# Set-up of a two-layer transformer kernel: seven staging buffers, block 0's attention first, later weight strips beside block 0's MLP

## The reference

```python
# layer 0
h = ada_rms(x, cond, ln1_w, ln1_tw)        # x*rsqrt(mean x^2) * w*(1 + cond @ tw.T)
q, k, v = h@Wq.T, h@Wk.T, h@Wv.T           # 8 query heads of 64, one k/v head
q, k = rope(q), rope(k)
x = x + softmax(q k^T / 8) v @ Wo.T
h = ada_rms(x, cond, ln2_w, ln2_tw)
x = x + (silu(h@Wg.T) * (h@Wu.T)) @ Wd.T   # 2048 inner
# layer 1
gamma1, gamma2, scale1, scale2, shift1, shift2 = silu(cond) @ Wada.T + bada
x = x + attn(ln(x)*(scale1+1)+shift1) * gamma1      # 16 heads of 32, unit q and k
x = x + (gelu(( ln(x)*(scale2+1)+shift2 )@Wfc1.T + bfc1)@Wfc2.T + bfc2) * gamma2
```

## Time and profile before

| | |
|---|---|
| runs | 2766.93, 2768.59, 2770.6 us (median 2768.59) |
| profiled execution, its own time | 2764.49 us |
| its span, first to last instruction | 2762.7 us |
| mean granted TensorE clock | 0.969 |
| TensorE busy | 2524.8 us, 91% |
| VectorE, ScalarE, GpSimd busy | 1395.9, 962.3, 1040.4 us |
| TensorE by 40 slices of 69 us | 2449999999999999999997769999999999999998 |
| granted clock by slice | 9669999999999999999999889999999999999999 |

### The profile page before, as it was taken

How to read it: one execution, slowest core, us unless ns; L and a number is a source line. 1 busy time by engine, 2 the same in 40 slices (tenths; PEclk the granted TensorE clock), 3 DMA queues, 4 the chain that set the end, 5 groups by cost and what they waited for, 6 DMA issues and landing times.

```text
span 2762.7 us, 47260 instructions
## 1 busy us (share of the span) xinstructions
PE 2524.8 (91%) x18552; PEld 1255.8 (45%) x18552; DVE 1395.9 (51%) x2115; ACT 962.3 (35%) x1549; POOL 1040.4 (38%) x1007
## 2 busy tenths in 40 slices
PE   2449999999999999999997769999999999999998
PEld 1224445454444444444443335454454545454543
DVE  4554434243342524435224657575767667575742
ACT  2332213132231322223122336262626354444532
POOL 1112223132231322223121546564655555565632
PEclk9669999999999999999999889999999999999999
DMA  6430010100001010010205111212121112112110
GB/s 201 132 98 3 7 45 3 50 3 28 26 5 48 3 46 7 12 40 4 76 3 179 36 43 29 74 31 76 28 66 44 55 42 60 48 45 65 32 54 27
DMA packets 115019, 129.40 MB, mean 47 GB/s; under 512 B 53758, under 2 KB 56190, under 8 KB 114820
## 3 DMA queue, kind: packets, MB, share of 16 engines
q1 hardware_dynamic: 114820, 126.36, 15.2%
HBM read 71.79 MB, written 18.87 MB: 33 GB/s over the span
## 4 chain that ended last, share of the span: by engine, by line
PE 73%; issue 10%; DVE 7%; POOL 5%; ACT 4%; DMA 0%; POOLq 0%; SPq 0%; DVEq 0%; ACTq 0%
PE ps_m L1440 38%; PE ps_abef L1440 18%; PE ps_d L1440 2%; PE ps_c L1440 2%; PE ps_abef L1619 2%; PE ps_abef L1621 2%; PE ps_abef L1626 2%; PE ps_abef L1653 1%; PE ps_d L1607 1%; POOL h_mlp L815 1%; POOL inner L837 1%; POOL scratch L868 1%; PE ps_abef L1642 1%; PE ps_abef L1661 1%; PE ps_c L1475 1%
## 5 line engine op out<-in xcount | busy, mean ns | idle before, releaser
L1440 PE MATMUL ps_m<-h_mlp,weights 128*128 128x512 f16 x3072 | 708.5, 383 | 38.9 <-POOL h_mlp L815 19.1
L1440 PE MATMUL ps_m<-weights,inner 128*128 128x512 f16 x3072 | 690.4, 379 | 8.7 <-DVE scratch L1280 8.7
L1440 PEld LDWEIGHTS ps_m<-h_mlp,weights 128*128 128x128 f16 x3072 | 296.8, 99 | 384.9 <-issue 38.4
L1440 PEld LDWEIGHTS ps_m<-weights,inner 128*128 128x128 f16 x3072 | 296.9, 98 | 346.1 <-DVE scratch L1280 6.5
L837 POOL TENSOR_TENSOR inner<-scratch,inner 128x512 f16<-128x512 f32 x256 | 301.0, 1176 | 315.6 <-ACT inner L1000 315.6
L1440 PE MATMUL ps_abef<-h_mlp,weights 128*128 128x512 f16 x1536 | 345.4, 379 | 0.0
L1440 PEld LDWEIGHTS ps_abef<-h_mlp,weights 128*128 128x128 f16 x1536 | 147.6, 98 | 173.0
L806 POOL TENSOR_TENSOR scratch<-scratch 128x1 f32<-128x1 f32 x128 | 29.1, 228 | 434.3 <-ACT scratch L945 379.1
L1000 ACT CAST inner<-scratch 128x512 f16<-128x512 f32 x256 | 156.6, 612 | 101.6 <-DVE scratch L1408 68.1
L815 POOL TENSOR_TENSOR h_mlp<-scratch,h_mlp 128x512 f16<-128x512 f32 x64 | 74.0, 1156 | 199.2 <-ACT h_mlp L958 199.2
L1278 DVE SCALAR_TENSOR_TENSOR scratch<-scratch,ps_m 128x512 f32<-128x512 f32 x64 | 44.0, 688 | 198.2 <-ACT scratch L1008 198.2
(11 more groups left out here) (169 smaller groups left out, 3646.3 us busy)
## 6 DMA issues: line engine op xcount, KB each, us to landing
x_mlp<-x_attn SPq DMA_DIRECT2D x64, 256.0 KB, 2.3
weights<-gamma SPq DMA_DIRECT2D x128, 128.0 KB, 2.9
scratch<-scratch SPq DMA_DIRECT2D x128, 128.0 KB, 2.6
x_attn<-x SPq DMA_DIRECT2D x32, 256.0 KB, 2.7
x_mid<-x_mlp SPq DMA_DIRECT2D x32, 256.0 KB, 2.0
x_attn<-x_mid SPq DMA_DIRECT2D x32, 256.0 KB, 2.7
out<-x_mlp SPq DMA_DIRECT2D x32, 256.0 KB, 2.2
inner<-wada_t SPq DMA_DIRECT2D x6, 1024.0 KB, 5.9
```

The source lines that it names most:

```text
L1440: ins = nc.tensor.matmul(o, left(a, k), right(b, k), start=(first and n == 0), stop=(last and n == len(order) - 1), skip_group_check=True)
```

## The change

It replaces the order of set-up by two tables, `SETUP_AT` (by slot of block 0's attention) and `START_AT` (by slot of block 0's MLP), whose pieces each engine takes at the head of a slot.

- Block 0's attention has a table of its own, `FIRST0`, with 20 slots: proj of the tiles in slots 2, 5, 8, 11, norm2 in 13, 15, 17, 19.
- Seven staging buffers: i0 to i3 in `inner`, b0 to b2 in the space of `down_w`, and the fourth quarter of that space for the modulation's results.
- The ada strips aren't cut. TensorE multiplies them in fp32, right from the staging buffer, into four PSUM banks in turn.
- The first eight sequences' gains are written straight into `gains`, and the rope rows of block 0 into `rope`. The angles are worked out in four parts (4, 8, 10 and 10 of 32 columns of 32).
- gate2, up2, gate3, up3 and down0 to down3 are cut in slots 1 to 8 of block 0's MLP; TensorE waits for each pair of up and gate strips only where it needs it, and ScalarE waits for all cuts before chunk 8, which overwrites i1.
- Loads wait by buffer, x has one semaphore a tile, POOL makes the frequencies first.

```diff
+GROUPS0 = ["tw0", "qkv", "qkv_v", "tw1", "wo", "gate0", "up0", "ada4", "ada5", "ada6", "ada7", "ada2", "ada3",
+           "gate1", "up1", "gate2", "up2", "gate3", "up3", "down0", "down1", "down2", "down3"]
+STAGED0 = ["i0", "i1", "i2", "i3", "b0", "b1", "b2", "i0", "i1", "i2", "i3", "b0", "b1",
+           "b2", "i1", "i3", "b0", "b1", "b2", "i1", "i3", "i1", "i3"]
+ADAS = [0, 1, 4, 5, 6, 7, 2, 3]
+SETUP_AT = {
+    0: [("ang", 0)],
+    1: [("sin", 0), ("ang", 1), ("ada", 0)],
+    2: [("cut", "qkv"), ("cut", "qkv_v"), ("store", 0), ("load", "gate0"), ("rope", 0), ("sin", 1), ("ang", 2)],
+    3: [("rope", 1), ("load", "up0"), ("sin", 2), ("load", "ada4"), ("ada", 1), ("store", 1)],
+    4: [("rope", 2), ("load", "ada5"), ("ang", 3), ("sin", 3)],
+    5: [("cut", "wo"), ("load", "ada6"), ("ada", 4), ("store", 4)],
+    6: [("rope", 3), ("load", "ada7"), ("ada", 5), ("store", 5)],
+    7: [("rope_out", 0), ("load", "ada2"), ("cut", "gate0"), ("ada", 6), ("store", 6)],
+    9: [("load", "ada3"), ("ada", 7), ("store", 7)],
+    10: [("cut", "up0"), ("ada", 2), ("store", 2)],
+    11: [("load", "gate1"), ("load", "up1"), ("load", "gate2")],
+    12: [("load", "up2"), ("ada", 3), ("store", 3)],
+    13: [("load", "gate3")],
+    18: [("cut", "gate1")],
+    19: [("cut", "up1")],
+}
+START_AT = {
+    0: [("load", "up3")],
+    1: [("cut", "gate2"), ("load", "down0")],
+    2: [("cut", "up2"), ("load", "down1")],
+    3: [("cut", "gate3")],
+    4: [("cut", "up3")],
+    5: [("cut", "down0")],
+    6: [("load", "down2"), ("cut", "down1")],
+    7: [("load", "down3"), ("cut", "down2")],
+    8: [("cut", "down3")],
+}
...
             def ada(n):
-                pe.wait_ge(s_wlo, g + 1)
...
-                    for f in range(KC):
-                        ins = products([(bank[:, NSEQ * f:NSEQ * (f + 1)], lambda b, k: c[:, b, k, :])],
-                                       lambda a, k: ada_cut[:, a, k, P * f:P * (f + 1)], range(KC))
+                    for f in range(KC):
+                        for k in range(KC):
+                            ins = nc.tensor.matmul(bank[:, NSEQ * f:NSEQ * (f + 1)], staged(g)[:, k, P * f:P * (f + 1)],
+                                                   c[:, k, :], start=(k == 0), stop=(k == KC - 1))
...
-            for s in range(SLOTS0):
-                for stage, t in TABLE0[s]:
+            for s in range(FIRST_SLOTS):
+                setup(SETUP_AT.get(s, ()))
+                for stage, t in FIRST0[s]:
                     attn0(stage, 0, t)
-                if FIRST + s < SETUP:
-                    setup_group(FIRST + s)
-            pe.wait_ge(s_wlo, SETUP)
+            pe.wait_ge(s_ada_out, len(ADAS))
...
+                            if first_block(it) and j % 4 == 0:
+                                pe.wait_ge(s_wlo, cut_no(no_of(f"up{j // 4}")))
...
+                if L is L0 and first_block(it) and j == IC // 2:
+                    act.wait_ge(s_wlo, cut_no(SETUP - 1))
```

More of the change, by code:

```diff
@@ L70, with table0 @@
                     [2, 6, 10, 14], [0, 4, 8, 12], [1, 5, 9, 13], [16, 18, 20, 22], [17, 19, 21, 23])
+FIRST_SLOTS = 20
+FIRST0 = slot_table(FIRST_SLOTS, ["proj", "turn", "scores", "softmax", "turn_p", "mix", "out"],
+                    [2, 5, 8, 11], [0, 3, 6, 9], [1, 4, 7, 10], [12, 14, 16, 18], [13, 15, 17, 19])
+def table0(it):
+    return FIRST0 if isinstance(it, int) and it == 0 else TABLE0
 def order_of(table, stages):
@@ L648, in _ @@
+            load_x(L0, x, 0, 0)
+            sp.dma_start(ln_w_t, ln_w).then_inc(s_lnw, 16)
+            for name in ("tw0", "qkv", "qkv_v"):
+                load_group(no_of(name))
+            for t in range(1, TILES):
+                load_x(L0, x, 0, t)
+            sp.dma_start(b_ada_t, b_ada).then_inc(s_bada, 16)
             for n in range(2):
-                sp.dma_start(b_ada_bc[n], b_ada_row[n:n + 1, :].to_broadcast([NSEQ, D])).then_inc(s_setup_dma, 16)
+                sp.dma_start(gamma_row[n], b_ada_row[n:n + 1, :].to_broadcast([NSEQ, D])).then_inc(s_bada, 16)
@@ new lines, in setup @@
+            def setup(pieces):
+                for piece, which in pieces:
+                    if piece == "load":
+                        load_group(no_of(which))
+                    if piece == "store":
+                        store_ada(which)
+                    if piece == "rope_out":
+                        sp.wait_ge(s_rope, len(ROPE_PARTS))
+                        rest = slice(TILES, NBLK * TILES)
+                        for which, table in ((0, cos_t), (1, sin_t)):
+                            sp.dma_start(rope_dram[:, rest, which, :],
+                                         table.rearrange("p (t f) -> p t f", f=32)[:, rest]).then_inc(s_rope_st, 16)
@@ L840, in _ @@
             pool.wait_ge(s_const, 43)
-            for s in range(SLOTS0):
-                for stage, t in TABLE0[s]:
+            for slot in FIRST0:
+                for stage, t in slot:
                     attn0(stage, 0, t)
@@ new lines, in setup @@
+            def setup(pieces):
+                for piece, which in pieces:
+                    if piece == "ang":
+                        angles(which)
+                    if piece == "rope":
+                        rotations(which)
+                    if piece == "ada":
+                        ada(which)
+                    if piece == "cut":
+                        cut_lo(no_of(which))
+            dve.wait_ge(s_pos, 16)
+            link(nc.vector.tensor_copy(pos_f, pos_i))
+            dve.wait_ge(s_const, 35)
```

384 lines of the change are left out of this document (196 added, 188 removed).

## The result

The changed kernel takes 2704.43 us (median of 4 runs, 2702.99 to 2707.65); the kernel before, run beside it, 2768.89 (4 runs, 2766.93 to 2770.6). The ratio is 0.9769, 95% interval 0.9752 to 0.9786. Forecast: 2707, range 2688 to 2727. The profiled execution took 2702.99 us, its span 2701.0 (before: 2762.7), so the spans differ by 61.7.

What follows compares the result with a forecast made beforehand. The prediction took TensorE's stream to bound the kernel, with set-up a hole at its front. Savings of 32.5 + 35 + 2 = 69.5 us, less 8, gave 61.5; from the 2768.6 median it forecast 2707, range 2688 to 2727.

Steps and rivals of the forecast that it cites:

- start, saved: Up to the first projection: it would start at 21.5 us in place of 54, saving 32.5.
- tile stretches, saved: Block 0's attention, proj of tile 0 to proj of tile 3: 106.0 us becomes 71, saving 35.
- tile 3 to the MLP, saved: Proj of tile 3 to block 0's MLP: 46.9 us becomes 45, counted as 2 saved.
- block 0's MLP, lost: Eight strips cut in slots 1 to 8 of block 0's MLP cost 8 us more.
- the rest: Per-tile x semaphores, renumbered cuts and waits of layer 1: long past events, so no cost.
- Price of the fp32 products: TensorE's ada products: between 1.8 and 9.1 us each, middle of 5.3 taken; 2.5 us not covered in the tile stretches.
- The lap: Block 0's MLP: ScalarE and VectorE's round per late cut takes 9.6 us against a slot's 6.8.
- A: Rival: the late cuts' relay binds at every slot of block 0's MLP, 22 us in place of 8; 15%.
- B: Rival: fp32 products dear, 9.1 us and more, adding 12 to 20 before the MLP; 15%.
- C: Rival: fp32 at its lower bound and late cuts hidden, total time 2688 to 2694 us; 14%.
- D: Rival: tiles keep their old pace of 34 to 36 us, only the start is won, 2744 us; 5%.
- E: Rival: slower than before, last strips arrive late, TensorE idle 8.7 us per strip decides; 2780 us if all eight; 2%.

Runs made afterwards that it cites:

- e1: Changed kernel with the cuts of qkv and its v columns moved ahead of ada0's finish and norm1 of tile 0: 2697.88 us, ratio 0.9744.
- e9: Changed kernel with the gains of block 0's first norm written to DRAM and loaded back again: 2710.7 us, ratio 0.9788.
- e10: Changed kernel with the fourth tile's angles, sine and rope row made in tile 2's slots: 2703.36 us, ratio 0.9766.
- e11: e8 with e10's edit added and ada4's product ten slots later: 2690.92 us, ratio 0.9717.
- e4: Changed kernel with the eight ada strips cut to fp16 pairs again and multiplied in fp16 passes: 2749.45 us, ratio 0.9939.
- e6: Changed kernel, fp32 products kept, with the ada strips cut all the same into space nobody reads: 2712.49 us, ratio 0.9803.
- e5: Kernel before the change with only the 20-slot table FIRST0 for block 0's attention: 2760.78 us, ratio 0.9976.
- e8: Changed kernel with e1's edit, late cuts behind each chunk's work, ada6 in slot 18, and gate1, up1, gate2 cut by halves: 2688.57 us, ratio 0.9719.
- e7: Changed kernel with every fp32 product of an ada strip done twice: 2717.21 us, ratio 0.9824.
- e2: Changed kernel with all eight late strips cut before slot 0 of block 0's MLP: 2715.81 us, ratio 0.9819.

## Why the prediction was right

The mechanism was right: set-up was the hole, and the strip's relay set the tiles' pace. The sizes err both ways. That their sum is off by only 0.2 us is luck: the terms are off by 2.7, 3.5, 0.8, 0.9 and 2.3.

| step | predicted | measured |
|---|---|---|
| start, saved | 32.5 | 29.85 |
| tile stretches, saved | 35 | 38.5 |
| tile 3 to the MLP, saved | 2 | 2.8 |
| block 0's MLP, lost | 8 | 7.1 |
| the rest | 0 | 2.3 longer, within its scatter |
| spans | 61.5 | 61.7 |

- **Start.** Two terms were too small: the landing (about 9 taken, 10.11 here), and ada0, 5.3 taken and 7.06 measured, the first work of TensorE and as long as the products at 1.2 GHz. The rest, 14.09 less 7.06, is 7.0 us; the prediction had 7.1. It had the cut of qkv behind h's high half as a given; e1 shows that its place was worth 4.5. A trip of the gains through DRAM costs 8.4 in the changed kernel by e9; what it took in the kernel before was not measured.
- **Price of the fp32 products.** Both measured values lie inside the bounds of 1.8 and 9.1, and neither is near the middle that was taken. The prediction gave one price where there are two, by what TensorE did just before. The middle was also reached by a wrong step: it took 57 ns a pass from the 48 fp16 products (2.74 us) and multiplied it by 1.45. But the four of the kernel before that have a clock record (the row of 81.68 us above is one) all ran at 0.50, half clock. Taken as four passes an instruction, an fp32 pass of 64 columns is 108 ns at half clock, 1.9 times fp16's 57, and 58 at full clock, 1.5 times fp16's 39 (0.63 us over 16). With 512 columns an fp32 product takes 0.91 us and an fp16 one 0.23, four times as much. By the rule of the Trainium skill that was cited ("FP8 and Floating Point Precision", TensorE Precision Notes) true fp32 takes four passes: the trace agrees, in the rows with 512 columns. The estimate of 6.8 us from the Trainium skill ("TensorE: Matmul & The Clock Gate", Weight-path perf modes and LDWEIGHTS) agrees with the 6.93 and 7.06 at half clock; the 3.74 at full clock is 3.1 below it.
- **Tile stretches.** 21, 24.5, 23 and 2.5 for products were predicted, 21.61, 25.83 and 20.08 came. The first was right by a partly wrong reading: the angles do hold the scores' and the gain's operations, but ada4's cold 6.9 us, given no place of its own there, ends at the same time (e10 moves the angles alone and gains nothing, e11 both and gains 4.4). The third was read 2.9 too long; there the granted clock is 1.00, where it was 0.65 before, and out takes 2.75 us (4.61 in e10 at 0.87). The prediction named no gain from a warmer TensorE. Whether that is all of it was not tested.
- **What gives the 38.5.** The prediction worked each stretch out anew and did not say which edit carries the saving. The runs do: TensorE's wait in order for a pair that nobody needed yet, about 35 of the 71 us (e4 less e6); the engines' time for the ada cuts, 8 to 11 (e6); the way over DRAM, 8 (e9); the table, about 6 in the old surroundings (e5). These were taken at different ends and need not add up. The mis-sized expectation of e4 (10 to 18) shows the danger of counting a removed cut by its own duration.
- **Tile 3 to the MLP.** Of gate1's cut, predicted to stand there with its whole 4.2 us, 1.41 us of the high half are on the chain (at 125.66), and the relay's last wait is 3.61 for the 2.7 of the earlier trace rows; cutting by halves in the relay's gaps was part of what e8 won here (44.15 to 40.87).
- **Block 0's MLP.** VectorE has 17.5 us more in the block and ScalarE 13.7 (18.4 and 15 predicted). The lap was right in kind and the sum close, but the place was wrong: 3.2 us at slot 6's product wait was expected, and the product waits rose by 0.7; TensorE lost it at its small attention steps, whose operands come from the same late engine.
- **Rivals.** A was not seen (7 us, not 22). B's 9.1 us a product did not occur, not even at half clock (6.9 to 7.1), and e7, with every product done twice, costs 12.8 in all. C's time was not reached by the change; e8 reaches 2688.6, but by other places for the cuts and products, not by C's cheap fp32. D fell: the stretches left 34 to 36 us; e4 is what D would have looked like. E fell: no cut of the late strips held up TensorE for 8.7 us; in e2, where cuts stand ahead of all slots, the down strips' loads do hold them.

## What to carry to other kernels

An engine that works in order pays for an operation by the wait in front of it, and everything queued behind pays too: before pricing a removed step by its duration, ask who stands in line for it, and test that by running the step with nobody reading its result. When a stretch doesn't move, look for a second thing that ends at the same time, and take both away before calling either free. Try work that is put into a pipelined loop behind the loop's own operations of that slot, on every engine that the loop waits for; here that was 3.7 us cheaper than ahead of them.

## What the runs showed of the hardware

- 16 fp32 products, 128x128 weights and 64 moving columns each (shown as 32 records), took 3.74 us at a granted clock of 1.00 (the 2.4 GHz level) and 6.93 at 0.50 (1.2 GHz). 48 fp16 products of that size took 2.74 us at 0.50, and 16 took 0.63 at 1.00.
- With 512 moving columns, at 1.00, four fp32 products took 3.65 us and twelve fp16 ones 2.75: 0.91 against 0.23 each.
- More TensorE work can cost less than its time: with each fp32 product doubled, the mean granted clock of block 0's first two tile stretches rose from 0.74 and 0.76 to 1.00 and 0.94, and seven further products, 3.7 to 7 us each when done once, cost 7.5 us together.
- A 128 KB store behind 1 MB loads in one queue took 6.76 us to land, where the 16 KB load issued once it had landed took 1.97.
